# A DLRM tower on one core: what the embedding gathers of a tile are paced by

## The reference

```python
e = stack([tbl_f[ids[:, f]] for f in 39 fields], axis=1)            # (2048, 39, 32)
conv1 = einsum('bid,bjd,ijk->bkd', e, e, W1)                        # 128 maps
hidden1, final1 = conv1[:, :64], conv1[:, 64:]
conv2 = einsum('bid,bjd,ijk->bkd', e, hidden1, W2)                  # 128 maps
z = sum over d of concatenate([final1, conv2], axis=1)              # (2048, 192)
h = relu(concatenate([z, dense], axis=1) @ W_top1 + b_top1)         # 512
h = relu(h @ W_top2 + b_top2)                                       # 256
y = h @ W_top3                                                      # (2048, 1)
```

## Time and profile before

| | us |
|---|---|
| median of 3 runs | 910.13 (909.83 to 913.68) |
| the profiled execution | 914.24 |
| its span, first to last instruction | 912.4 |
| TensorE matmul busy | 807.8 (89%) |
| VectorE busy | 742.2 (81%) |
| ScalarE busy | 590.0 (65%) |
| GpSimd busy | 477.0 (52%) |
| mean granted TensorE clock | 0.966 of full speed |

### The profile page before, as it was taken

How to read it: one execution, slowest core, us unless ns; L and a number is a source line. 1 busy time by engine, 2 the same in 40 slices (tenths; PEclk the granted TensorE clock), 3 DMA queues, 4 the chain that set the end, 5 groups by cost and what they waited for, 6 DMA issues and landing times.

```text
span 912.4 us, 16542 instructions
## 1 busy us (share of the span) xinstructions
PE 807.8 (89%) x6012; PEld 476.5 (52%) x6012; DVE 742.2 (81%) x1252; ACT 590.0 (65%) x1567; POOL 477.0 (52%) x448
## 2 busy tenths in 40 slices
PE   2999958789989898998989888989899998999997
PEld 1566513244646555554645454555565564656576
DVE  5999969788888879777888878898968778889951
ACT  1343325737777777667676767777776767698883
POOL 6876656646665656555555556666555556500000
PEclk9999979989999899889999999999989899999999
DMA  5376978888888977767687887888767768786300
GB/s 130 135 156 181 274 197 231 247 256 232 255 251 252 261 210 212 216 161 223 186 248 201 244 221 218 219 224 256 204 196 207 210 181 241 193 246 198 113 1 1
DMA packets 140118, 184.54 MB, mean 202 GB/s; under 512 B 109539, under 2 KB 120191, under 8 KB 122053
## 3 DMA queue, kind: packets, MB, share of 16 engines
q1 hardware_dynamic: 123836, 174.34, 65.6%
q0 software_dynamic: 14208, 7.30, 5.7%
q10 hardware_dynamic: 1992, 1.85, 0.6%
HBM read 170.20 MB, written 18.21 MB: 206 GB/s over the span
## 4 chain that ended last, share of the span: by engine, by line
ACT 44%; PE 28%; another core or an unknown queue 14%; issue 5%; SPq 4%; DMA 3%; DVE 2%; ACTq 0%; DVEq 0%
ACT arena L610 24%; PE hidden L420 9%; ACT xdiag L598 9%; PE hidden L511 9%; ACT hid_high L581 6%; PE sums L445 4%; ACT hidden L587 3%; SPq L340 3%; PE sums L462 2%; DMA copies<-xt 2%; DVE blocks L753 1%; ACT act L631 1%; PE sums L487 1%; PE sums L477 1%
## 5 line engine op out<-in xcount | busy, mean ns | idle before, releaser
L386 POOL DMA_INDIRECT emb<-in_tbl,ids_tile x444 | 476.8, 1074 | 319.0 <-PE hidden L420 208.5
L753 DVE TENSOR_TENSOR blocks<-copies 117x512 f32<-117x512 f32 x840 | 523.7, 690 | 127.4 <-PE hidden L420 103.1
L420 PE MATMUL hidden<-blocks,w_pairs 117*64 117x512 f32 x1792 | 431.5, 613 | 19.2 <-DVE blocks L753 15.4
L610 ACT ACTIVATE arena<-sums 64x480 f32<-64x480 f32 (+2 forms) x936 | 293.0, 313 | 209.6 <-remote 153.4
L420 PEld LDWEIGHTS hidden<-blocks,w_pairs 117*64 117x64 f32 x1792 | 148.6, 139 | 226.9 <-issue 144.9
L445 PEld LDWEIGHTS sums<-xdiag,turned 64*103 64x103 f32 x2000 | 101.6, 171 | 125.7 <-issue 81.8
L445 PE MATMUL sums<-xdiag,turned 64*103 64x78 f32 x2000 | 115.2, 261 | 47.3 <-ACT arena L610 25.4
L598 ACT ACTIVATE xdiag<-turned 32x468 f32<-32x468 f32 (+1 forms) x256 | 118.8, 464 | 4.0 <-DVE turned L729 0.9
L462 PE MATMUL sums<-arena,weights 128*128 128x128 f32 x640 | 85.5, 287 | 6.9 <-issue 6.1
L581 ACT ACTIVATE hid_high<-hidden 32x512 f32<-32x512 f32 x128 | 75.2, 588 | 16.3 <-PE hidden L420 10.6
L462 PEld LDWEIGHTS sums<-arena,weights 128*128 128x128 f32 x640 | 77.4, 197 | 10.6 <-issue 7.6
(11 more groups left out here) (49 smaller groups left out, 405.3 us busy)
## 6 DMA issues: line engine op xcount, KB each, us to landing
copies<-xt SPq DMA_DIRECT2D x448, 312.0 KB
emb<-in_tbl,ids_tile POOLq DMA_INDIRECT x444
blocks<-hot_t SPq DMA_DIRECT2D x12, 500.0 KB
xt<-emb SPq DMA_DIRECT2D x32, 152.0 KB
xt<-xt SPq DMA_DIRECT2D x16, 304.0 KB
xt<-emb SPq DMA_DIRECT2D x32, 104.0 KB
hot_kept_rows<-rows SPq DMA_DIRECT2D x6, 480.0 KB
emb<-hot_kept_rows SPq DMA_DIRECT2D x15, 192.0 KB
```

What stands on the lines that cost most here:

```text
L386: pool.indirect_dma_start(out=emb[u][:, f * D:(f + 1) * D], out_offset=None, in_=tables[f], in_offset=bass.IndirectOffsetOnAxis(ap=ids_til ...
L420: mm = nc.tensor.matmul(hidden[64 * c:64 * c + 64, k % 2, bank, :], w_pairs[0:ROWS, t, bank * HALF_HID:bank * HALF_HID + HID], blocks[0:RO ...
L610: op = nc.scalar.activation(out[:, :, cols].rearrange("p h (u b) -> p h u b", u=2), g[rows, i], ACT.Copy)
L753: op = nc.vector.tensor_tensor(blocks[0:ROWS, at + c, :], a[:, cols], b[:, cols], ALU.mult)
```

## The change

A new semaphore, `strides`, is raised by TensorE 44 times in a full tile: by the first matmul (c = 0) of each of the 28 pairs, once in the middle of each Gram group (6), twice in each third of the final sums (6), and twice in each of the first two layers (4). Tile 0 has 31 of them and tile 1 has 40, since less work of earlier tiles lies in them. Gather `at` now waits for stride 1 + at x 44 // 27 of tile T-2, and not for pair at + 1. The increments on `hid_pairs` and all other waits stay.

```diff
+        strides = sem("strides")
+        def strides_of(tile):
+            sums, layers = 2 * THIRDS, 2 * 2
+            return PAIRS_A_TILE + N_GROUPS * (1 if tile == 0 else 2) + (sums if tile else 0) + (layers if since(tile, 2) else 0)
+        def strides_until(tile):
+            return sum(strides_of(t) for t in range(tile))
...
                     if at:
-                        pool.wait_ge(hid_pairs, pairs_done(2 * (tile - 2), 0, 0) + at * PAIRS_A_TILE // GATHERS)
+                        pool.wait_ge(strides, strides_until(tile - 2) + 1 + at * strides_of(tile - 2) // GATHERS)
                     gather(u, f)
...
@@ hidden_step, after the matmul of c
+                        if c == 0:
+                            mm.then_inc(strides, 1)
...
@@ gram_group, after both halves of place r
+                    if r == GROUPS[j] - 1 and chunk < CHUNKS - 1:
+                        mm.then_inc(strides, 1)
...
@@ final_sums, after matmul n
+                    if n - first in (2, 7) and tile < TILES - 1:
+                        mm.then_inc(strides, 1)
...
@@ layer1, after the first matmul of m
+                    if m % 2 and tile < TILES - 2:
+                        mm.then_inc(strides, 1)
...
@@ layer2, after matmul c of m
+                        if c == 1 and tile < TILES - 2:
+                            mm.then_inc(strides, 1)
```

More of the change, by code:

```diff
@@ L459, in final_sums @@
                 n_all = FH + F1
-                for n in range(n_all * j // 3, n_all * (j + 1) // 3):
+                first = n_all * j // 3
+                for n in range(first, n_all * (j + 1) // 3):
                     if n < FH:
@@ L476, in layer1 @@
                 for m in range(T1 // P):
-                    nc.tensor.matmul(outs1[:, m, :], wt1a[:, m * P:(m + 1) * P], z_conv2[:, :],
-                                     start=True, stop=False)
+                    mm = nc.tensor.matmul(outs1[:, m, :], wt1a[:, m * P:(m + 1) * P], z_conv2[:, :],
+                                          start=True, stop=False)
+                    if m % 2 and tile < TILES - 2:
+                        mm.then_inc(strides, 1)
                     mm = nc.tensor.matmul(outs1[:, m, :], wt1b[0:FIN1 + DENSE, m * P:(m + 1) * P], z_rest[:, :],
```

## The result

The changed kernel takes 863.36 us (median of 4 runs, 859.99 to 866.00), the kernel before 910.74 us beside it (4 runs, 909.83 to 913.68): a ratio of 0.9472, 95% interval 0.9429 to 0.9515. The prediction was 909.4 us, no change. That was wrong by 46 us. The profiled execution took 859.99 us, its span 858.2 us.

What follows compares the result with a forecast made beforehand. The prediction took TensorE, with small losses to ScalarE and VectorE, to bound the regular stretch. Its terms, -0.7 + 0 + 0, took 914.24 us (profiled) to 913.5, or the median of 910.13 to 909.4; range 902.5 to 917 us.

Steps and rivals of the forecast that it cites:

- What bounds the kernel: Regular stretch, 230 to 820 us: set by TensorE with small losses to ScalarE and VectorE; gathers lie beside it.
- Part 1: Gathers on GpSimd: same number, starts moved, last one 0.9 us later; cost 0, bounds 0 to 12.6 us.
- That gathers would still come in bursts: Rival on GpSimd: gathers stay in bursts, 910.1 us; counted inside the forecast's case, together 0.60.
- Part 2: VectorE's multiplies beside gathers: evenly spread gathers slow them less; 0.7 us gained, bounds 7.1 us gained and 0.
- Part 3: TensorE's 687 added semaphore increments: cost 0, bound 6.9 us.
- Fewer tiles at a lower clock: Rival on TensorE's clock: two of five slowed tiles lose their 3.3 us loss, 6.7 us less, 902.7 us; chance 0.14.
- All contention goes: Rival on VectorE: multiplies fall to 682 ns and TensorE uses it all, 7.1 us less, 903 us; chance 0.07.
- the test that I set: Full-clock tiles still take 47 to 49 us; a change above 0.3 us would show the forecast's mechanism wrong.
- the forecast of no change: Whole kernel: 909.4 us from the median of 910.13, counted as same within 0.5%; chance of same 0.60.

Runs made afterwards that it cites:

- e2: Kernel before without the gathers of tiles 2 to 15, an 8-column memset in each one's place, waits kept: 835.98 us, ratio 0.924.
- e1: Changed kernel with its 687 increments kept, but gathers waiting for pairs again as before: 906.68 us against 906.83, ratio 0.9995.
- e3: Kernel before with a 512-column GpSimd memset behind each gather from tile 2 on, waits as before: 894.36 us, ratio 0.990.
- e6: Changed kernel with a 128-column GpSimd memset behind each gather: 880.15 us, ratio 0.964 to the kernel before.
- e7: Changed kernel with gathers grouped in runs of three, same count and mean pace: 924.88 us, ratio 1.015 to the kernel before.
- e8: Changed kernel with gathers grouped in runs of nine, same count and mean pace: 1172.47 us, ratio 1.282 to the kernel before.
- e4: Kernel before with gathers waiting for Gram thirds, meant to move runs of the same length elsewhere: 922.50 us, ratio 1.020.

## Why the prediction was wrong

**What bounds the kernel: the step that failed.** "So the regular stretch is set by TensorE with its small losses to ScalarE and VectorE, and the gathers lie beside it." I had asked who waits for GpSimd, and no row names it as a releaser. But a wait is put down to the engine that raises the count, and a delay of the count on its way has no name. It stood in the profile: ScalarE's 134.5 us "remote", the longest wait of an engine that others wait for, and 14% of the chain for "another core or an unknown queue", in a kernel that runs on one core. I read neither. e2 sizes the step: gathers cost 71 us of 907, where I had 0 for their delay and 7.1 us as the most for all they do.

**Part 1, the move of the gathers.** The counting was right where it can be checked: SyncE shows no wait on a gather, and VectorE's waits for copies are 4.3 us from 230 to 775 us. But the cost of 0, with bounds of 0 and 12.6 us, is a term that moving gathers can only raise; that moving them might gain time by itself was not among the cases. This is the term where the 46 us are missing. GpSimd's idle time fell to 246.5 us and did not stay at 319, since the whole is shorter and a gather's instruction took 1125 ns and not 1074. That gathers would still come in bursts was a rival of mine, and it half came true (121 of 311 in runs of four or more).

**Part 2, VectorE.** The mechanism is small, as forecast: 691 ns became 686 ns a multiply (300 to 700 us), forecast 689. But the bound of "7.1 us over 14 tiles, the most that a better place for gathers could give" was far too low: a better place gave 47 us. The cheapest check was in hand: the tile from 789.7 to 833.5 us, the only regular one nearly without gathers (the last starts at 795.3), took

```profile
789.70:833.50 43.80, 42.36 (x341) 26.04 (x340) 39.73 (x67) 36.08 (x97) 3.46 (x4) 1.00 0.76 221
```

43.8 us, 4 us under the full-clock mean of 47.85. I used that stretch for the length of a multiply and not for the length of the tile. Times 14 it is 57 us, by estimate.

**Part 3, the increments.** Right: cost 0 within the interval of e1.

**The rivals.** "Fewer tiles at a lower clock" came true beside it: one of eleven and not five, 12.4 us of the 48.9. That it follows from the shorter waits is argued, not shown. I had said that "nothing in the change touches the waits for ScalarE", and it was just these that it touched. "All contention goes" was the right direction with a wrong mechanism and about a seventh of the size. Of the test that I set, "if they change by more than 0.3 us the forecast's mechanism is wrong": full-clock tiles changed by 3.3 us.

On the two other chips on which the changed kernel was timed against before, the forecast of no change would have held. That is luck and no credit to its reasoning, which knew nothing of the delay.

## What to carry to other kernels

Compare a stretch that has an engine's work with one that has not, before calling that engine harmless: who waits for it is no measure of what it costs. A large wait on an unnamed releaser ("remote", "unknown queue") in a one-core program is to be explained first; look how long after the producer's last instruction the waiter starts. Indirect DMAs issued by GpSimd beside a dense TensorE program are best spread out by what they wait on, which cost nothing on the two chips where it gained nothing; added work as a spacer did cost (e3, e6). A gain of this kind should be timed on more than one chip. And a trace that lacks records can make a count look late: in e7 eight rises are missing, and the next one comes 7.4 us later or more, while ScalarE had started within 0.05 us of the matmuls' end.

## What the runs showed of the hardware

While GpSimd's indirect DMAs of 128 rows ran back to back (one each 1.25 us), the count raised at the end of a train of short TensorE matmuls rose 2.1 us after the last one's start, against 0.27 us without them; half the rows changed nothing (1.96 us). In the same kernels the count was nearly on time where no gather ran beside the train (0.50 us in the changed kernel, 0.28 us in e8). In the midst of a run of ten it took 9.4 us from the end of the train until its waiter started, and TensorE's own issue fell to one weight load in 0.7 us. The counts of pairs, whose matmuls take 0.43 us each, were hardly late in the kernel before (VectorE, where it waited, started 0.15 us in the median after the pair's last matmul, 0.12 us without gathers), but up to 4.9 us in e7 and 8.4 us in e4. The same program took 907 to 918 us on the chip with this behaviour and 847 to 850 us on three chips without it.
